# A gather that zeroes its row buffers once, masks unknown ids by a factor, and has its GpSimd loop written out

## The reference, cut to what matters

```python
for i in range(4):
    left, right = (CUTOFF_ENDS[i], CUTOFF_ENDS[i + 1])      # 0, 5000, 15000, 25000, 32000
    mask = (flat >= left) & (flat < right)
    idx = jnp.clip(flat - left, 0, right - left - 1)
    e = jnp.einsum('td,pd->tp', tables[i][idx], projs[i])
    out = out + jnp.where(mask[:, None], e, 0.0)
out = out * EMB_SCALE                                        # 16
h = h + _L0_attn_ref(_layernorm(h), ...)                     # projections, convolution, state-space scan
h = h + _L0_ffn_ref(_layernorm(h), ...)                      # shared and routed experts
```

## Time and profile before

| | us |
|---|---|
| median of 3 runs (461.7 to 462.69) | 461.78 |
| the profiled execution | 461.5 |
| its span on the core | 459.7 |
| TensorE busy | 405.5 (88%) |
| VectorE busy | 291.1 (63%) |
| ScalarE busy | 238.1 (52%) |
| GpSimd busy | 223.6 (49%) |

### The profile page before, as it was taken

How to read it: one execution, slowest core, us unless ns; L and a number is a source line. 1 busy time by engine, 2 the same in 40 slices (tenths; PEclk the granted TensorE clock), 3 DMA queues, 4 the chain that set the end, 5 groups by cost and what they waited for, 6 DMA issues and landing times.

```text
span 459.7 us, 8621 instructions
## 1 busy us (share of the span) xinstructions
PE 405.5 (88%) x2880; PEld 356.7 (78%) x2880; DVE 291.1 (63%) x626; ACT 238.1 (52%) x433; POOL 223.6 (49%) x284
## 2 busy tenths in 40 slices
PE   2756899999688797489999999999999999998996
PEld 1645788889566796269888888898988898987885
DVE  6597687988965667986556455466365455565333
ACT  4255677777567433553453553554545544634442
POOL 5777767773693005553824634535545347244000
PEclk9898999999979888889999999999999999999999
DMA  2314294111089998210120120120130021100101
GB/s 51 98 54 146 90 314 152 61 52 50 24 261 296 222 224 296 66 47 0 47 66 27 46 93 1 46 91 0 46 92 9 37 91 46 46 0 0 47 0 46
DMA packets 32683, 38.86 MB, mean 85 GB/s; under 512 B 3301, under 2 KB 28867, under 8 KB 32528
## 3 DMA queue, kind: packets, MB, share of 16 engines
q1 hardware_dynamic: 29600, 33.25, 24.6%
q0 software_dynamic: 3056, 5.26, 3.9%
HBM read 34.56 MB, written 8.65 MB: 94 GB/s over the span
## 4 chain that ended last, share of the span: by engine, by line
PE 65%; DVE 14%; POOL 7%; issue 6%; ACT 3%; DMA 2%; POOLq 0%; SPq 0%; DVEq 0%; ACTq 0%
PE ps L1078 19%; PE ps L1079 19%; PE ps L1080 19%; DVE hid_lo L1009 3%; DMA toep_l<-kernel_rows_dram 2%; POOL cat L529 2%; POOL rstd L536 2%; PE ps L1161 2%; DVE hn L901 2%; PE ps L1116 1%; PE ps L1197 1%; DVE toep_r L856 1%; DVE h2n L901 1%; PE ps L1086 1%; DVE sw_lo L956 1%
## 5 line engine op out<-in xcount | busy, mean ns | idle before, releaser
L1009 DVE SCALAR_TENSOR_TENSOR hid_lo<-act_out,hid_hi 128x512 fp32r<-128x512 f32 x64 | 56.6, 886 | 55.8 <-ACT hid_hi L791 55.8
L778 ACT ACTIVATE act_out<-ps,vec 128x512 f32<-128x512 f32 x32 | 22.1, 689 | 91.6 <-PE ps L1080 91.6
L1003 DVE SCALAR_TENSOR_TENSOR act_out<-ps,vec,act_out 128x512 f32<-128x512 f32 x32 | 24.0, 750 | 53.9 <-ACT act_out L778 53.9
L536 POOL TENSOR_TENSOR rstd<-rstd,minus_half 128x1 f32<-128x1 f32 x64 | 37.9, 592 | 40.9 <-DVE rstd L897 39.8
L529 POOL DMA_INDIRECT cat<-table_dram,idx x32 | 38.1, 1191 | 26.9 <-POOL idx L525 19.1
L613 POOL TENSOR_TENSOR h_sb<-h_sb,bias_e 128x256 f32<-128x256 f32 x32 | 24.5, 768 | 53.6 <-DVE h2n L901 53.6
L1080 PE MATMUL ps<-h2nT_hi,sw_lo 128*128 128x512 f32 x128 | 50.0, 391 | 0.0
L1079 PE MATMUL ps<-h2nT_lo,sw_hi 128*128 128x512 f32 x128 | 50.0, 391 | 0.0
L1078 PE MATMUL ps<-h2nT_hi,sw_hi 128*128 128x512 f32 x128 | 49.9, 390 | 0.0
L606 POOL TENSOR_TENSOR zc_lo<-v_sb,zc_hi 128x256 fp32r<-128x256 f32 x32 | 29.4, 920 | 35.0 <-ACT zc_hi L768 34.9
L782 ACT ACTIVATE act_out<-ps,vec 128x512 f32<-128x512 f32 x32 | 22.1, 689 | 40.6 <-PE ps L1080 40.5
(11 more groups left out here) (127 smaller groups left out, 1277.6 us busy)
## 6 DMA issues: line engine op xcount, KB each, us to landing
toep_l<-kernel_rows_dram SPq DMA_DIRECT2D x6, 1024.0 KB, 11.6
h_rows_dram<-h_ring SPq DMA_DIRECT2D x32, 128.0 KB
toep_r<-kernel_rows_dram SPq DMA_DIRECT2D x4, 1024.0 KB, 6.3
h_in<-h_rows_dram SPq DMA_DIRECT2D x8, 512.0 KB, 4.4
stage<-w_e_dram POOLq DMA_DIRECT2D x7, 512.0 KB, 3.6
out_dram<-o_sb SPq DMA_DIRECT2D x7, 512.0 KB, 3.2
toep_r<-kernel_rows_dram SPq DMA_DIRECT2D x4, 512.0 KB, 9.0
bias_e<-rows_dram SPq DMA_DIRECT2D x1, 1024.0 KB
```

Of the source, the lines that this page charges most:

```text
L536: nc.gpsimd.tensor_tensor(rstd[:, m:m + 1], rstd[:, m:m + 1], minus_half[:, :], ALU.pow).then_inc(s_rstd, 1)
L778: nc.scalar.activation(act_out[:, n % 4, :], ps[bank][:, :], ACT.Silu, bias=vec[:, C_SB1 + j:C_SB1 + j + 1]).then_inc(act_done, 1)
L1003: nc.vector.scalar_tensor_tensor(act_out[:, n % 4, :], ps[bank + 1][:, :], vec[:, C_SB3 + j:C_SB3 + j + 1], act_out[:, n % 4, :], ALU.add, ...
L1009: nc.vector.scalar_tensor_tensor(hid_lo[:, n % 4, :], act_out[:, n % 4, :], 0.5 if kind == SHARED else 0.25, f32(hid_hi[:, n % 4, :]), ALU ...
```

## The change

- `idx` and its copy are gone; the indirect DMA takes its ids from `x_ids` directly.
- The eight row buffers are zeroed once, by eight memsets of VectorE that now stand ahead of its other two. Rows of ids outside the vocabulary then keep what an earlier tile left in them.
- VectorE makes `mask` (128 x 32) with two instructions, 16 for an id inside the vocabulary and 0 for one outside. They stand between the memsets and the wait for the small vectors.
- `h_out` multiplies by the mask's column, one factor per token, where it multiplied by the constant 16. The instruction is an `activation` with a per-partition scale in place of a `mul` with an immediate.
- A gather waits for `cat_tr` (TensorE has turned the tile eight before) where it waited for `catT_lo_done` (VectorE has split it), which comes later.
- GpSimd's four groups are written out in Python; the `Fori` and the register arithmetic of its waits are gone.

```diff
-    idx = sb(mem_a, "idx", [P, RES], I32, L)
+    mask = sb(mem_a, "mask", [P, GROUPS, RES], F32, L)
...
         def gather(i, r):
-            n = RES * i + r + 1
-            if not isinstance(i, int) or i:
-                need(pool, catT_lo_done, n - RES, half_set)
-            nc.gpsimd.memset(cat[:, r, :], 0.0).then_inc(cat_zero, 1)
-            if isinstance(i, int) and i == 0 and r == 0:
+            n = RES * i + r
+            if i:
+                pool.wait_ge(cat_tr, n - RES + 1)
+            else:
+                pool.wait_ge(cat_zero, r + 1)
+            if n == 0:
                 pool.wait_ge(ids_in, 16)
-            nc.gpsimd.tensor_copy(idx[:, r:r + 1], x_ids[:, bass.ds(i, 1), r:r + 1].rearrange("p o r -> p (o r)")
-                                  ).then_inc(idx_copied, 1)
-            need(pool, idx_copied, n, half_set)
-            need(pool, cat_zero, n, half_set)
             pool.indirect_dma_start(cat[:, r, :], None, table,
-                                    bass.IndirectOffsetOnAxis(ap=idx[:, r:r + 1], axis=0),
+                                    bass.IndirectOffsetOnAxis(ap=x_ids[:, i, r:r + 1], axis=0),
                                     bounds_check=VOCAB - 1, oob_is_err=False).then_inc(gathered[r], 16)
...
-        group(0)
-        with pool.Fori(1, GROUPS - 1) as i:
+        for i in range(GROUPS):
             group(i)
-        group(GROUPS - 1)
...
-            nc.scalar.mul(h_ring[:, r % 4, :], EMBP[r % 2][:, 0:D], EMB_SCALE).then_inc(h_done, 1)
+            if isinstance(i, int) and n == 0:
+                act.wait_ge(mask_step, 2)
+            in_vocab = mask[:, bass.ds(i, 1), r:r + 1].rearrange("p o r -> p (o r)")
+            nc.scalar.activation(h_ring[:, r % 4, :], EMBP[r % 2][:, 0:D], ACT.Identity, scale=in_vocab).then_inc(h_done, 1)
...
     def _(dve):
+        for r in range(RES):
+            nc.vector.memset(cat[:, r, :], 0.0).then_inc(cat_zero, 1)
         nc.vector.memset(x_pad[:, :, :, :], 0.0).then_inc(pad_zero, 1)
...
+        dve.wait_ge(ids_in, 16)
+        all_ids = x_ids[:, :, :].rearrange("p g r -> p (g r)")
+        all_mask = mask[:, :, :].rearrange("p g r -> p (g r)")
+        nc.vector.tensor_scalar(all_mask, all_ids, float(VOCAB), EMB_SCALE, ALU.is_lt, ALU.mult).then_inc(mask_step, 1)
+        dve.wait_ge(mask_step, 1)
+        nc.vector.scalar_tensor_tensor(all_mask, all_ids, 0.0, all_mask, ALU.is_ge, ALU.mult).then_inc(mask_step, 1)
         dve.wait_ge(vec_in, 16)
```

More of the change, by code:

```diff
@@ L187, in _tower @@
     bias_step = sem("bias_step")
-    idx_copied = sem("idx_copied")
     cat_zero = sem("cat_zero")
+    mask_step = sem("mask_step")
     gathered = [sem(f"gathered{r}") for r in range(RES)]
@@ L540, in group @@
             for r in range(RES):
-                if r or not isinstance(i, int) or i:
+                if r or i:
                     power_step(RES * i + r - 1, (r - 1) % 4, eps_done, rstd_done)
@@ L544, in group @@
                     gather(i, r + LEAD)
-                elif not isinstance(i, int) or i + 1 < GROUPS:
+                elif i + 1 < GROUPS:
                     gather(i + 1, r + LEAD - RES)
-                if isinstance(i, int) and i == 0 and r in (4, 6):
+                if i == 0 and r in (4, 6):
                     m = (r - 4) // 2
```

## The result

The changed kernel takes 457.82 us (median of 4 runs, 455.83 to 459.17) against 462.24 before (also 4 runs; the prediction reckoned from the three it had, 461.78): ratio 0.9895, interval 0.9852 to 0.9939, so 4 to 5 us faster. That is clear of the noise (2.8 us at the least), though under 2%. The prediction said 455.6, range 453.0 to 459.5.

A forecast was written before the change was run, and what follows sets the result against it. GpSimd's gather steps and VectorE were taken to bound phase A ahead of 62.7 us, TensorE after. 2.1 + 1.4 + 0.9 + 1.2 + 1.0 - 0.4 = 6.2 us gave 455.3, stated as 455.6, range 453.0 to 459.5 (own 454.2 to 457.5).

The forecast's parts named there:

- What bounds the front, and that the rest is shifted: Phase A: only time ahead of 62.7 us can change; TensorE is full until 113.65 and everything behind shifts as a whole.
- GpSimd's step: Gather loop ahead of 62.7 us: removing memset and copy shortens each position from 3.10 to 2.5 us.
- the lead-in: Idle time ahead of each gather on GpSimd, 0.80 to 0.98 us; taken as the gather's own, so about 0.8 stays.
- rival 2: Ahead of gathers: the idle time goes with the copy, GpSimd's step falls to 1.7 us, about 453.5 us; chance 0.10.
- VectorE's head: Start of VectorE's list: memsets and mask delay the powers 2.4 us, yet the lead is 2.1, then 3.5 us at 23.30.
- The cover: VectorE's wait for GpSimd's first power step hides the added 2.1 us, which would otherwise cost in full.
- From 23.30 to 41.14: VectorE's own work stays; shorter waits for GpSimd's queue gain 0.9 us, bringing the lead to 4.4.
- From 41.14 to 62.70: Two positions at GpSimd's faster pace gain 1.2 us until 48.61; then TensorE's wait gives 1.0 back, lead 6.6.
- TensorE's wait: Single wait of 1.11 us at 62.69, whose chain ran over GpSimd; 1.0 us expected back.
- ScalarE: `h_out` with scale from memory: 0.095 us more per instruction, about four times on the path, costing 0.4 us.
- The rule on the shared port: VectorE's port hold could delay six early gathers up to 0.6 us each, 3.6 us, giving 457.0; chance within rival 1's.
- rival 1: In the head VectorE becomes the bound, the 2.1 us arrive in full; gain 2.8, time 459.0; chance 0.20.

The follow-up runs named there:

- e4: Changed kernel with GpSimd zeroing the row buffer ahead of each gather, no memsets on VectorE, ids still read from x_ids: 459.45 us, ratio 0.9929.
- e10: Kernel before the change with 2.8 us more of memsets at the start of VectorE's list: 464.03 us, ratio 1.0024.
- e2: Changed kernel with the eight row buffers zeroed on GpSimd ahead of the first gather instead of on VectorE: 456.62 us, ratio 0.9854.
- e1: Changed kernel with GpSimd's weight split one position earlier: 455.48 us, ratio 0.9813.
- e6: Changed kernel with the weight split ahead of the gather instead of behind it, at the same positions: 453.95 us in one run.
- e8: Changed kernel with the constant 16 back as scale, the mask made but not applied: 457.45 us, ratio 0.9882.
- e9: Changed kernel with the row buffers released by catT_lo_done, as before, in place of cat_tr: 457.67 us in one run.
- e5: Changed kernel with GpSimd's chain of bias instructions held back until VectorE's last convolution of phase A: 452.84 us, ratio 0.9798.
- e3: Changed kernel with the copy of the ids to idx put back ahead of each gather: 460.82 us, ratio 0.9927.
- e0: Changed kernel, unaltered, run again as the reference for the first set: 459.11 us, ratio 0.9892.
- e7: Changed kernel with weight split one position earlier, buffers zeroed by GpSimd up front and bias chain held back, together: 447.52 us, ratio 0.9678.

## Why the prediction was right, and where its steps were off

- **What bounds the front, and that the rest is shifted:** right. 4.1 us of lead stand where TensorE is full (the turn of tile 16 at 60.67 against 64.75 in the chain of waits), 3.8 at the end of the span.
- **GpSimd's step:** mis-sized. 2.5 us were forecast, 1.8 measured. By the reading at e4 the lead-in is the gather's own, as I took it, but I left it exposed, while it now runs beside the instruction in front. By the prediction's own signs ("I am wrong if the lead-in is gone or grows") this step was wrong: 0.18 to 0.30 us of 0.80 to 0.98 are left to see. That is rival 2 on GpSimd, though not in its price, as VectorE bounds.
- **VectorE's head:** 2.9 us for eight memsets, measured 3.4 (1.01 to 4.41); `catT_lo` of tile 0 at 10.7, measured 10.51. The cover held: first `shift` 17.3 forecast, 16.86 measured, lead at the second 3.5 forecast, 4.05 measured. e10 bears out that the wait covers it; e2 says what remained: once GpSimd is faster, VectorE's head is the bound and the memsets there cost about 2 us.
- **From 23.30 to 41.14:** this step failed. I wrote that VectorE's own work stays and took 0.9 us more of lead, 4.4 in sum; measured 1.96. What I left out is that VectorE could be held: two `shift`s are held for 1.8 us each until GpSimd's weight split ends. In the kernel before the split never met a `shift`; the faster gather moved it onto one. e1 takes the holds away, 3.6 us in sum, and the first projection comes 2.9 us earlier; e6 shortens them by 2.6. Without them the gain is above the forecast's 6.2: e1's ratio is worth 8.6 us (interval 7.0 to 10.3).
- **From 41.14 to 62.70:** 1.2 forecast, 0.62 measured (2.58 - 1.96); then 1.0 forecast for TensorE's wait, 1.50 measured (4.08 - 2.58).
- **ScalarE:** 0.095 us per instruction forecast, 0.090 measured; 0.4 on the path fits e8, within its error.
- **The rule on the shared port:** I weighed it for the gathers and found its case a rival at 457.0. The changed kernel's early gathers last 1.00 to 1.24 us in its own profile, so there it did not show. But in e6 and e8, whose heads are the same, one gather lasts 1.74 and 1.78 us, beside a VectorE instruction with two operands in SBUF:

```profile
9.57 0.96 DVE L878 TENSOR_TENSOR proj_lo<-toep_r,proj_hi 128x768 fp32r<-128x768 f32 x1
```
```profile
9.66 1.74 POOL L526 DMA_INDIRECT cat<-table_dram,x_ids  x1 [0.30 <-issue]
```

  In the changed kernel's profile this gather starts 0.04 us ahead of that instruction (9.60, 9.64). In e9 it starts 0.04 us behind it and still lasts 1.00, so the order alone does not decide. It cost nothing, since GpSimd waits for VectorE at the first power step anyway (3.19 us in the changed kernel, 2.03 in e6). It showed the other way round, where I had not looked: GpSimd's split and its scaling of `bias_e` hold VectorE's `shift` and its last normalization. The Trainium skill ("SBUF — State Buffer", the same passage) says so too, for VectorE instructions that have two inputs in SBUF or run in a mode that uses both port pairs: whoever is first keeps the pair for the whole instruction and the other blocks fully. e6 agrees to 0.02 us, e5 with 5.1 us. The changed kernel itself agrees only in part: its `shift` started 0.6 us ahead of the split and was held all the same. The 5.49 us of the earlier trace rows had stood in my own rows as a thing that stays, and not as a warning.

So the time came 2.2 us above the 455.6 that I forecast: inside the range, but 0.3 above the 457.5 at which the forecast's own range ended. The cheaper gather step gave a little (0.55 us of lead more than forecast at the second `shift`), and a collision that stands in none of my terms and rivals took some 3 us back. That a miss of this size stayed inside 459.5 is luck: that end was set for rival 1, VectorE's head arriving in full, which did not happen.

## What to carry to other kernels

When an engine gets faster, list what now runs beside what: a wide GpSimd instruction can hold a VectorE instruction that works on SBUF, and a tiny one on the critical chain can be held for the length of the wide one. Not every VectorE instruction is held: here `shift` (two inputs in SBUF) and a normalization of 128 x 256 were, while the sum over states, the two small instructions that prepare `rstd`, and `catT_lo`, which reads PSUM and one tile in SBUF, kept their usual time beside the split (kernel before, 31.97 to 33.24; e1). Put GpSimd's wide work beside such work. And let an indirect DMA wait for nothing that its own engine has just done: the 0.8 us ahead of it then run beside the instruction in front (0.18 to 0.31 us left to see, against 0.80 in e3 and e4).

## What the runs showed of the hardware that I had not expected

- A VectorE instruction of 128 x 1 elements lasted 1.92 us beside a GpSimd instruction of 1.29 us: the hold began 0.6 us before GpSimd's recorded start, while a gather ran in front of it. With no such instruction queued behind it, the same gather held nothing (e1). What holds it so early stays open.
- GpSimd's eight memsets in a row held a VectorE instruction of 0.12 us for 1.20 us (e2), past the end of the single memset that ran when it came.
- TensorE's pace in the front differs between runs with no edit to explain it. Of the nine profiles of the changed kernel and of e0 to e7, seven had another granted clock between 16 and 46 us than the kernel before (0.77 to 1.00 against 0.89). Ahead of 16 us the clock column says 1.00 in every profile, and yet the matmuls of `embed` last 0.41 us at first and 0.28 later, from 13.99 us on in e6, 16.40 in the changed kernel and 17.20 in e0; the first `shift` starts at 15.99 in e6 and at 16.86 in the other two. The column does not show this change of pace. What decides when they change was not found.
